# The wedge measure of the first batch on ScalarE and GpSimd instead of VectorE, in an attention and mixture-of-experts block

## What is computed

```python
qp = _linear(hidden_states, Wtq, btq)                  # two coordinates for each token
diff = qp[:, :, None, :] - qp[:, None, :, :]
dist_sq = jnp.sum(diff * diff, axis=-1)
phase_diff = jnp.arctan2(diff[..., 1], diff[..., 0])
forward_bias = 0.5 * (1.0 + jnp.cos(phase_diff))
...
valid = (dist_sq <= threshold) & causal[None]
binary_attn = valid.astype(scores.dtype) * forward_bias
masked = jnp.where(binary_attn == 0, -jnp.inf, scores)
weights = jax.nn.softmax(masked, axis=-1)
```

## Time and profile before

| What | Value |
|---|---|
| median of 3 runs | 710.03 us (708.62 to 712.08) |
| the profiled execution's own time | 709.09 us |
| its span, first to last instruction | 707.4 us |
| busy over the span | PE 83%, DVE 79%, ACT 56%, POOL 54% |
| mean granted clock of TensorE | 0.941 of full speed |
| first batch's attention, from the first chunk to the first routing part | 76.6 to 181.2 us |

### The profile page before, as it was taken

The page is one execution under the profiler, slowest core; times in us unless marked ns, Lnnn a source line. Parts: engine busy times, 40 slices in busy tenths (PEclk is TensorE's granted clock), DMA queues, the critical chain, the costliest instruction groups (busy, mean ns, idle before and its releaser), DMA issues. The chain is left out here.

```text
span 707.4 us, 11540 instructions
## 1 busy us (share of the span) xinstructions
PE 590.4 (83%) x3660; PEld 334.4 (47%) x3660; DVE 558.3 (79%) x1519; ACT 396.8 (56%) x793; POOL 384.3 (54%) x343
## 2 busy tenths in 40 slices
PE   1766978897678898899989999799788588989895
PEld 1634445565452533434445445454354355555553
DVE  3478799996879899678778777678976988888886
ACT  0522566686434755467867878665455354545452
POOL 8359455937504343879776577543234355555553
PEclk9995689898869999999989999999999999999999
DMA  7201001100000000000000000000000000000000
GB/s 192 65 1 33 1 0 34 35 0 1 1 1 0 2 0 1 16 1 1 1 16 1 1 2 0 17 1 1 0 1 17 0 2 16 1 16 2 16 1 17
DMA packets 14052, 9.14 MB, mean 13 GB/s; under 512 B 1556, under 2 KB 12840, under 8 KB 13992
## 3 DMA queue, kind: packets, MB, share of 16 engines
q1 hardware_dynamic: 13992, 8.41, 4.1%
HBM read 6.31 MB, written 2.10 MB: 12 GB/s over the span
## 5 line engine op out<-in xcount | busy, mean ns | idle before, releaser
L546 POOL TENSOR_TENSOR gp<-stage,gp 128x512 f16<-128x512 f32 x144 | 166.9, 1159 | 226.8 <-ACT gp L702 215.5
L702 ACT CAST gp<-stage 128x512 f16<-128x512 f32 x144 | 88.3, 613 | 84.5 <-DVE stage L1482 83.2
L689 ACT ACTIVATE stage<-bank 128x512 f32<-128x512 f32 x144 | 84.7, 588 | 28.0 <-PE bank L747 27.8
L894 PE MATMUL bank<-v,ptr 128*128 128x128 f32 x544 | 79.1, 288 | 1.9 <-DVE x L1255 1.9
L651 ACT COPY ptr<-bank 128x512 f32<-128x512 f32 (+2 forms) x80 | 41.5, 518 | 69.7 <-PE bank L879 68.9
L894 PEld LDWEIGHTS bank<-v,ptr 128*128 128x128 f32 x544 | 72.9, 204 | 4.1 <-ACT ptr L651 1.6
L1406 DVE SCALAR_TENSOR_TENSOR hid<-stage,bank 128x512 f32<-128x512 f32 x72 | 49.0, 681 | 30.6 <-ACT stage L689 30.6
L1482 DVE SCALAR_TENSOR_TENSOR stage<-bank,stage 128x512 f32<-128x512 f32 x72 | 49.7, 691 | 26.1 <-ACT stage L689 24.1
L745 PE MATMUL bank<-wd,gp 128*128 128x128 f16 x288 | 52.5, 221 | 20.4 <-POOL gp L546 17.2
L1464 DVE SCALAR_TENSOR_TENSOR ysb<-bank,comb,ysb 128x128 f32<-128x128 f32 x240 | 67.1, 343 | 0.0
L745 PE MATMUL bank<-h,wg 128*128 128x512 f16 x144 | 55.9, 388 | 11.9 <-DVE hid L1406 11.5
(11 more groups left out here) (269 smaller groups left out, 1400.6 us busy)
## 6 DMA issues: line engine op xcount, KB each, us to landing
out_x<-x SPq DMA_DIRECT2D x8, 256.0 KB, 2.3
stage<-in_L_ffn_gate_w SPq DMA_DIRECT2D x1, 576.0 KB, 7.4
stage<-in_L_ffn_up_w SPq DMA_DIRECT2D x1, 576.0 KB, 4.2
stage<-in_L_ffn_down_w SPq DMA_DIRECT2D x1, 576.0 KB, 4.1
stage<-in_L_ffn_gate_w SPq DMA_DIRECT2D x1, 448.0 KB, 7.2
stage<-in_L_ffn_up_w SPq DMA_DIRECT2D x1, 448.0 KB, 3.5
stage<-in_L_ffn_down_w SPq DMA_DIRECT2D x1, 448.0 KB, 3.5
row<-in_L_wmod SPq DMA_DIRECT2D x1, 384.0 KB
```

The lines of the kernel that those rows point to most:

```text
L546: pool.tensor_tensor(gp[:, s % 3, 1, :], act_g[:, s % 2, :], gp[:, s % 3, 0, :], ALU.subtract)\
L689: act.activation(sg[:, s % 2, :], gate_bank(s)[:, :], func, scale=half_of / (H_UP * W_UP))\
L702: act.copy(gp[:, (s - 1) % 3, 0, :], act_g[:, (s - 1) % 2, :]).then_inc(act_high, 1)
L894: last = mm(ring(b, 3, i)[:, 0:P], ptr[:, m % 2, k * P:(k + 1) * P], v[:, j, :], start=(j == 0), stop=(j == i))
```

## The change

The bound `POOL_FROM` goes. All 40 chunks of the first batch's attention are measured as the second batch's are: 32 more shifts on ACT and 32 more subtractions on POOL, in the slots that `MEASURES_AT` gives, and 32 instructions L1269 fewer on DVE. Nothing else is moved by the text; in POOL's queue each measure stands ahead of the slot's root, `base` part and `split`.

```diff
-POOL_FROM = CHUNKS_BEFORE[14]
...
-        def by_pool(b, m):
-
-            return b > 0 or m >= POOL_FROM
-
         def pooled(b, m):
 
-            return b * NCH + m - POOL_FROM + 1
+            return b * NCH + m + 1
...
-                if k == PIECES - 1 and b:
+                if k == PIECES - 1:
                     for m in range(2):
                         measure(b, m)
 
             def attention(b, n):
                 for m in MEASURES_AT.get(n, ()):
-                    if by_pool(b, m):
-                        measure(b, m)
+                    measure(b, m)
...
-                if by_pool(b, m):
-                    if pooled(b, m) > 2:
-
-                        act.wait_ge(measure_ready, pooled(b, m) - 2)
-                    act.wait_ge(rise_ready, NCH * b + m + 1)
-                    act.activation(dx[:, pooled(b, m) % 2, 0:w], xb[:, lot], ACT.Identity, bias=nxi[:, i:i + 1])\
-                       .then_inc(dx_ready, 1)
+                if pooled(b, m) > 2:
+
+                    act.wait_ge(measure_ready, pooled(b, m) - 2)
+                act.wait_ge(rise_ready, NCH * b + m + 1)
+                act.activation(dx[:, pooled(b, m) % 2, 0:w], xb[:, lot], ACT.Identity, bias=nxi[:, i:i + 1])\
+                   .then_inc(dx_ready, 1)
...
-                    if by_pool(b, n):
-                        dve.wait_ge(measure_ready, pooled(b, n))
-                    else:
-                        lot = slice(c * W, min((c + 1) * W, L))
-                        dve.wait_ge(rise_ready, NCH * b + n + 1)
-                        step(dve.scalar_tensor_tensor(out=o[:, lot], in0=xb[:, lot], scalar=nxi[:, i:i + 1],
-                                                      in1=o[:, lot], op0=ALU.add, op1=ALU.subtract, reverse1=True))
-                        settle()
+                    dve.wait_ge(measure_ready, pooled(b, n))
```

## The result

| | before | after |
|---|---|---|
| median of the runs beside each other | 709.33 us (4 runs) | 721.25 us (4 runs) |
| the same, a second set | 708.74 us (23 runs) | 718.95 us (6 runs) |
| profiled execution, its span | 709.09, 707.4 us | 722.09, 720.4 us |
| busy: PE, DVE, ACT, POOL | 83%, 79%, 56%, 54% | 83%, 75%, 58%, 57% |

The changed kernel is slower: ratio 1.0163 with a 95% interval of 1.0122 to 1.0203, and 1.0170 (1.0137 to 1.0203) in the second set. The medians lie 11.9 and 10.2 us apart, and the ratios come to 11.6 and 12.0 us; the prediction said 6.2.

The account below looks back on a forecast made before the run. The prediction took DVE, with PE close behind, as the limit before, and POOL's queue order after. It added 0 + 6.2 us of POOL idling to the median of 710.03 us: 716.2 us, own range 713 to 719, whole range 709.5 to 723.

Parts of the forecast that it names:

- The signs that it named: In 77 to 180 us: POOL over 90% busy, DVE about 60%, three DVE waits of 4 to 6 us behind splits.
- the signs of being wrong: DVE waiting mainly for PE, long POOL waits for DVE in slots 16 and 29, or routing beginning before 182 us.
- The sum of POOL's queue: POOL's work in slots 0 to 35: measures 44.0, base 33.6, roots 4.8, splits 27.6, in all 110.0 us.
- POOL's waits for ACT: POOL's idle time in the first batch's attention: 1.2 at the beginning, 0.7, 3.6, and 0.7 at chunk 38, together 6.2 us.
- With a POOL that never waits, the change is worth nothing, and each microsecond that POOL idles is lost: POOL's queue up to routing: the change gains 0 us without waits, and idling between 77.6 and 178 us is lost time.
- ACT's supply behind the split of slot 17: From there to chunk 34's measure ACT needs 26.3 us against POOL's 22.7, so POOL idles 3.6 us.
- From chunk 37 to routing: Without POOL waits chunk 37's measure ends at 178.2 us, DVE takes about 1.5 us a chunk, routing begins at about 180.
- The 1.2 us set down for the last split beside the routing: Routing's gain of 1.2 us is taken back, since POOL's last split lies wholly beside the first part of routing.
- The second rival: DVE and PE run dry in three splits, TensorE falls to half clock: 9.6 us on top, 719 to 726 us, chance 0.20.
- the fast rival: In the chunk loop DVE's relief comes through and ACT's 94.9 us become the bound: 703 us, chance 0.05.
- The rest of the program, +0 assumed: Everything behind the start of routing moves by the same amount as routing; the second batch's program is unchanged.

Follow-up runs that it names:

- shift_only: The changed kernel, but for the first 32 chunks of the first batch ACT makes the shift and DVE subtracts, with none of those measures on POOL: 715.08 us, ratio 1.0071.
- base_and_splits: The changed kernel with base group 1 ahead of POOL's first measure and the four weight splits in slots 36 to 39: 727.63 us (one execution).
- copies_dve: The changed kernel with the first batch's copies of the transposed probabilities on DVE instead of ACT: 719.26 us, ratio 1.0128.
- dx_deep: The changed kernel with six buffers for the shift in the first batch instead of two: 714.83 us.
- base_early: The changed kernel with group 1 of base put ahead of the first measure on POOL: 715.28 us, ratio 1.0079.
- mixed: The kernel before with eleven more chunks, about every second one and none right behind a weight split, on ACT and POOL: 706.93 us, ratio 0.9980.
- late_start: The kernel before with 15 idle reductions on DVE ahead of the first batch's attention, which started 11.25 us later: 721.71 us.
- from10: The kernel before with POOL_FROM at chunk 10 instead of 32, so only chunks 0 to 9 stay on DVE: 715.76 us, ratio 1.0102.
- splits_late: The changed kernel with the four weight splits moved from slots 8, 17, 30 and 34 to slots 36 to 39, behind all measures: 730.71 us.

## Why the prediction was right in kind and short in size

- **Direction and mechanism: right for the stage.** DVE's relief brought nothing, and POOL's queue order is the largest part of the loss. Of the 8.6 us of the stage, taking POOL's 32 measures away (shift_only) brought back 7.8, putting 11.2 us of `base` ahead 4.3, putting the splits behind 4.2, and these two together 6.3.
- **The signs that it named: not all met.** POOL was busy 100.5 of 112.2 us from 77.66 us to routing, 90%, and DVE 62%. But DVE's long waits were 4.8 us behind `base` and 3.5 us behind the first split, and not three of 4 to 6 us behind the splits. And DVE waited 18.8 us for TensorE's distance term and only 14.5 for POOL's measures, which the prediction had put among the signs of being wrong. TensorE's own work wasn't the bound, though, since its weight loads waited 14.5 us for ACT's exponential:

```profile
PEld bank L872 <- ACT row L650: 14.5, 18, 2.7
```

- **The sum of POOL's queue: right in its numbers.** 110.0 us and 6.2 us idle from 77.6 us put the end of the last measure at 193.8 us; it was 193.50 + 1.39 = 194.9, and 192.6 in the repetition, which had begun 2.1 us earlier. POOL's waits for ACT came to 8.7 us and not 6.2: 0.9, 1.1 and 3.8 in the first three stretches (1.2, 0.7 and 3.6 were forecast) and 2.8 behind the third root (0.7). The start of POOL's work on the first measure was 77.66. The timeline of after shows its durations unstretched, and no wait for DVE at the third root:

```profile
77.66 0.46 POOL L504 TENSOR_TENSOR row<-row,dx 128x128 f32<-128x128 f32 x1 [12.44 <-ACT dx L587]
...
169.69 1.01 POOL L446 TENSOR_TENSOR rs<-ve,minus_half 128x4 f32<-128x4 f32 x1
...
181.82 1.27 POOL L504 TENSOR_TENSOR row<-row,dx 128x512 f32<-128x512 f32 x1 [0.29 <-ACT dx L587]
185.57 1.27 POOL L504 TENSOR_TENSOR row<-row,dx 128x512 f32<-128x512 f32 x1 [2.48 <-ACT dx L587]
186.80 2.10 POOL L455 TENSOR_TENSOR wd<-stage,w_up 128x1152 f16<-128x1152 f32 x1
...
193.50 1.39 POOL L504 TENSOR_TENSOR row<-row,dx 128x512 f32<-128x512 f32 x1
```

- **"With a POOL that never waits, the change is worth nothing, and each microsecond that POOL idles is lost": wrong as a rule.** It took the queue as binding from end to end. Where it was relieved of some 25 us (base_and_splits), the stage became 6.3 us shorter, and removing 6.9 us from the third stretch saved less than one. The queue binds in the first two stretches, and the third hangs on ACT as long as POOL makes the measures (copies_dve). That the prediction's account still came out near is in part luck: both engines were nearly full there, 33.34 and 34.29 us of 38.04.
- **ACT's supply behind the split of slot 17, 3.6 us: the right place, engine and size.** POOL's four waits there come to 3.8 us. I had begun the count with ACT standing still for want of a buffer. Six buffers (dx_deep) didn't shorten the third stretch (38.4 us), so it is ACT's work in that stretch.
- **From chunk 37 to routing: mis-sized, 1.8 us forecast and 6.8 measured (3.0 before).** I let DVE take 1.5 us a chunk behind the measures, with routing 1.8 us behind the end of chunk 37's. In after it waited for TensorE in most chunks from 32 on, the first of them at half clock, as before. From its timeline:

```profile
174.94 0.69 DVE L1261 SCALAR_TENSOR_TENSOR pen<-bank,row 128x512 bf16<-128x512 f32 x1 [4.82 <-PE bank L847]
...
186.29 0.69 DVE L1261 SCALAR_TENSOR_TENSOR pen<-bank,row 128x512 bf16<-128x512 f32 x1 [0.78 <-PE bank L847]
188.47 0.69 DVE L1261 SCALAR_TENSOR_TENSOR pen<-bank,row 128x512 bf16<-128x512 f32 x1 [0.69 <-PE bank L847]
```

  Chunk 37's measure was done at 183.1 us (183.7 by the forecast's terms) and its penalty begins at 188.47, so it lay ready for 5.4 us. The queue reached this point where it was forecast, but routing didn't hang on it: it began at 189.9 us and not at about 187, and the stage lost 8.6 us and not 6.2. That the sum of POOL's queue came so near is luck in this part. The 1.2 us set down for the last split beside the routing didn't arise, since from routing to the fourth root it took 26.9 us in both kernels. The better way to have reckoned is from the third root: 22.0 us to routing before, 20.2 in after, in its repetition and in six of the variants (within 0.1 us).
- **The second rival (TensorE's clock by way of the root's wait): not as it was put.** POOL waited for DVE at no root, which was its point of decision. The clock was lower in the first stretch, 0.70 against 0.80, and part of its 5.2 us may be that. In base_early it was 0.79 and in base_and_splits 0.82, so it went with the waits for POOL there. No run separates the two.
- **The Trainium skill's rule** ("Perfetto Trace Analysis", "Optimizing Scalar/DVE Operations"), that work may well go from a saturated DVE to ScalarE or even GpSimd, would have given the fast rival's 703 us. These runs bear it out at best in a small dose (mixed, 0.998, with no change inside its interval). Its own warning, that a move between DVE and GpSimd might not help, fits the outcome, but the reason that it gives, the shared read port, isn't what the runs show here: the time followed the order and the load of the two receiving queues.
- **The rest of the program, +0 assumed: not settled.** Over both sets of after the median is some 11.6 us above before, and the stage accounts for 8.6 and 8.5 us in two traces. What remains is some 3 us with the same instructions behind the routing. From routing to the fourth root it took 26.9 to 27.0 us in before, in after and in every variant that moves neither the splits nor the copies (27.2 in late_start), so the difference lies behind that root. From there to POOL's next root of four columns (`rs`, 128x4) the same piece of program took 320.9 us (mixed) to 335.3 (from10): 322.8 in before, 327.1 and 324.7 in after, but 322.5 in base_early and 321.9 in splits_late and base_and_splits, which have the same measures on POOL. After's two traces differ there by a stretch at half clock. A later start is unlikely to be the cause (late_start). Whether after's median is higher there by the clock's chance or for a reason that the traces don't show stays open.

The range of 709.5 to 723.0 held the time. The forecast's own range of 713 to 719 did not hold the first set's 721.25, and just held the second's 718.95.

## What to carry to other kernels

Work that moves to an engine with idle time must be read against that engine's queue: which long pieces stand ahead of it, and whether the idle time lay where the new pieces are due. Here 43 us were free on POOL, but part of them only because `base` had run ahead of time, which it no longer could behind measures that came late; and behind a weight split of 7 us DVE waited 3.5 us for a measure the first time and 1.2 us the second. And a stage in which four engines are 60 to 90% busy can have a different limit in each stretch: relieve one engine at a time before giving the loss to one cause. Measure each trace from the stage's own start, and look whether the event at which you cut is released by the same engine in both kernels. Here the start moved by 2.1 us between two executions, and the third root by 3.1 us against DVE's asking.

## What the runs showed of the hardware that was not expected

- Two executions of the same program parted by 2.1 us ahead of the stage and by 2.3 us in a later stretch of some 325, each with a lower granted clock of TensorE in one of them (0.73 against 0.91 in 68 to 74 us, 0.50 against 1.00 in 301 to 306 us), while the stage between them repeated within 0.2 us (113.2 and 113.0). Ten runs of one kernel (dx_deep) lay from 712.7 to 722.7 us. A difference of 3 us between the times of two single traces of this kernel is no finding.
- The stretching of DVE's instructions beside POOL's (L1269 from 0.74 to 2.85 us in before) was some 9 of the 30 us that left DVE, and its going brought no time, since DVE was no longer the limit. What was left of it on DVE showed up still: L1235, the half-precision split of the second layer norm, took 2.52 us at 108.60 us in after, beside POOL's weight split, against 0.71 at the same place before.
